# One more pass of lag in a normed attention whose token-major rows have two buffers

## What is computed

```python
qkv = (x @ qkv_w + qkv_b)            # 12 heads of 64
q = layernorm(q, q_norm_w, q_norm_b) # over the 64 features of a head
k = layernorm(k, k_norm_w, k_norm_b)
attn = softmax(q * scale @ k.T)      # 36 x 36 for each head and image
o = (gates[..., None] * (attn @ v)).reshape(B, N, H * HD)
return o @ proj_w + proj_b           # added to the stream h
```

## Time and profile before

| | |
|---|---|
| median of 3 runs | 762.44 us (762.32 to 763.35) |
| the profiled execution, its own time | 763.16 us |
| its span | 761.4 us |
| A1, from token_major(0) to turn(stage + 1, 0) | 271.5 to 390.9 us of the span |
| mean granted TensorE clock | 0.946 of full speed |
| busy: PE, DVE, ACT, POOL | 708.0, 494.7, 345.8, 164.4 us |

### The profile page before, as it was taken

How to read it: one execution, slowest core, us unless ns; L and a number is a source line. 1 busy time by engine, 2 the same in 40 slices (tenths; PEclk the granted TensorE clock), 3 DMA queues, 4 the chain that set the end, 5 groups by cost and what they waited for, 6 DMA issues and landing times.

```text
span 761.4 us, 15938 instructions
## 1 busy us (share of the span) xinstructions
PE 708.0 (93%) x6222; PEld 626.6 (82%) x6222; DVE 494.7 (65%) x1231; ACT 345.8 (45%) x800; POOL 164.4 (22%) x164
## 2 busy tenths in 40 slices
PE   7799999999998799899899998999999999999996
PEld 6588898999985666688776787889999867789996
DVE  1748478888777836466553674478666768456784
ACT  0257354555452133576423432355544545247653
POOL 1200036444242021334111000016443220000000
PEclk9899999999999879899799997999999999769998
DMA  9912022223220000000200010032130200112100
GB/s 263 251 55 79 2 56 77 77 77 104 94 64 0 1 0 2 2 2 1 96 1 1 2 43 2 1 100 58 58 114 23 86 1 3 50 38 74 36 22 24
DMA packets 16200, 38.81 MB, mean 51 GB/s; under 512 B 3577, under 2 KB 4569, under 8 KB 15740
## 3 DMA queue, kind: packets, MB, share of 16 engines
q1 hardware_dynamic: 14150, 36.71, 16.6%
q10 hardware_dynamic: 1976, 1.08, 0.6%
HBM read 37.32 MB, written 0.44 MB: 50 GB/s over the span
## 4 chain that ended last, share of the span: by engine, by line
PE 68%; DVE 20%; issue 4%; POOL 3%; ACT 3%; DMA 1%; POOLq 0%; ACTq 0%; DVEq 0%; SPq 0%
PE PS L711 7%; PE PS L767 5%; PE PS L543 4%; PE PS L547 4%; PE PS L545 4%; PE PS L544 4%; PE PS L546 4%; PE PS L659 4%; PE PS L700 3%; PE PS L595 3%; PE PS L732 2%; POOL ssq L1767 2%; DVE AL L1438 2%; PE PS L596 2%; PE PS L597 2%
## 5 line engine op out<-in xcount | busy, mean ns | idle before, releaser
L936 ACT ACTIVATE MIX<-PS 128x288 f32<-128x288 f32 x118 | 48.5, 411 | 114.8 <-PE PS L547 114.6
L543 PE MATMUL PS<-XH,WH 128*128 128x288 f32 x284 | 87.3, 307 | 2.2 <-DVE OT L1427 1.4
L545 PE MATMUL PS<-XH,WL 128*128 128x288 f32 x284 | 84.7, 298 | 0.0
L544 PE MATMUL PS<-XL,WH 128*128 128x288 f32 x284 | 84.7, 298 | 0.0
L546 PE MATMUL PS<-X,WH 128*128 128x288 f32 x284 | 84.6, 298 | 0.0
L547 PE MATMUL PS<-X,WL 128*128 128x288 f32 x284 | 84.5, 298 | 0.0
L1740 POOL TENSOR_TENSOR rstd<-var,nhalf 96x3 f32<-96x3 f32 x18 | 15.3, 849 | 305.5 <-DVE var L1195 305.5
L1427 DVE TENSOR_TENSOR OT<-MIX,PS 128x288 f32<-128x288 f32 x94 | 42.3, 451 | 39.7 <-ACT MIX L936 39.0
L1438 DVE TENSOR_TENSOR AL<-OT,AH 128x288 fp32r<-128x288 f32 x118 | 59.0, 508 | 3.3 <-ACT AH L950 2.3
L1281 DVE TENSOR_TENSOR WL<-RG,WH 128x768 fp32r<-128x768 f32 (+2 forms) x46 | 57.9, 1258 | 4.4 <-ACT WH L916 4.3
L595 PE MATMUL PS<-AH,DW 128*128 128x288 f32 x166 | 52.6, 317 | 7.2 <-DVE AL L1438 7.0
(11 more groups left out here) (234 smaller groups left out, 1687.8 us busy)
## 6 DMA issues: line engine op xcount, KB each, us to landing
RG<-in_gu_l0f_dram SPq DMA_DIRECT2D x8, 512.0 KB, 4.6
RG<-in_gu_l0f_dram SPq DMA_DIRECT2D x16, 256.0 KB, 5.7
RG<-in_gu_l2f_dram SPq DMA_DIRECT2D x9, 384.0 KB, 3.5
RG<-in_gu_l2f_dram SPq DMA_DIRECT2D x18, 192.0 KB, 4.3
RD<-in_wd_l0f_dram SPq DMA_DIRECT2D x8, 384.0 KB, 3.2
RD<-in_wd_l2f_dram SPq DMA_DIRECT2D x9, 288.0 KB, 2.8
RD<-in_wd_l3f_dram SPq DMA_DIRECT2D x6, 384.0 KB, 3.2
BIG<-in_patch_dram SPq DMA_DIRECT2D x6, 288.0 KB, 7.5
```

What stands on the lines that cost most here:

```text
L543: mm(o, WH[r][:, 0, w], XH[:, cols], start=True, stop=False)
L544: mm(o, WH[r][:, 0, w], XL[:, cols], start=False, stop=False)
L545: mm(o, WL[r][:, 0, w], XH[:, cols], start=False, stop=False)
```

## The change

The lag of the normed attention becomes 2, in the loops of all three engines, and on DVE normalised_heads moves from behind shift to the front of the next pass. The number of TX buffers stays 2 (the diff's new field txs is not read anywhere). The A1 loop has 18 passes; first_out stays 13, since it is the larger of 6 + 2 + 4 and 12 + 1. The other attentions keep their lag and order.

DVE's order in pass i is then: normalised_heads(i - 1), mean_square(i), shift(i - 3), norm(i - 4). PE does qk(i - 2), scores(i - 3), turn_probs(i - 5) and mix(i - 6) in pass i. ScalarE's copy of unit i into TX[i % 2] waits, as before, for qk(i - 2); that is now a step of the same pass.

```diff
         self.paired = dim == 16
-        self.lag = 1 if token_major else 0
+        self.lag = 2 if qk_norm else 1 if token_major else 0
+        self.txs = 2 if qk_norm else 2
...
                     act.wait_ge(S["qk_ready"], u0 + u - 1)
                     activation(TX[u % 2][:, :], PSF[0:TP, 1024:1024 + TAU * 256], ACT.Copy).then_inc(S["tm_taken"], 1)
 
-                lag = 1 if a.tm else 0
+                lag = a.lag
                 for i in range(a.units + lag + 4):
...
-                lag = 1 if a.tm else 0
+                lag = a.lag
                 for i in range(a.units + lag + 4):
+                    if a.qk_norm and 1 <= i <= a.units:
+                        normalised_heads(i - 1)
                     if a.qk_norm and i < a.units:
                         mean_square(i)
...
                     if 0 <= i - lag - 1 < a.units:
                         shift(i - lag - 1)
-                    if a.qk_norm and i < a.units:
-                        normalised_heads(i)
                     if a.gated and i == 0:
                         gates(a)
                     if 0 <= i - lag - 2 < a.units:
```

## The result

The first comparison gave 758.9 us as the median of four executions of the changed kernel (752.72, 752.96, 764.84, 770.68) beside 762.58 for the kernel before; the ratio is 0.9871, with a 95% interval of 0.9847 to 0.9894. Executions of one kernel here can differ by 17 us and more, and each ratio in this text leaves out those that lie over 1.5% above the shortest of their kernel, so it is a ratio of the shorter ones of each group; medians are given beside it, over all executions.

A forecast was written before the change was run, and what follows sets the result against it. The prediction held that a DVE-POOL loop set A1's settled passes (5.68 us, PE 5.15). Its terms, -2.6 - 5.0 - 6.8 + 5.1 + 3.9 = -5.4, took the profiled 763.16 to 757.8, median 757.0; range 753.2 to 761.6.

The forecast's parts named there:

- Settled passes, -2.6: token_major(6) to (11): five passes fall from 5.68 to 5.15 us, PE instead of the DVE-POOL loop setting the pace; -2.6 us.
- The new wait, 0: ScalarE's copy into TX waits for qk of its own pass; in settled passes 0.3 us of cover, no cost.
- The lock on POOL's side: DVE's norm beside POOL's power: its last two instructions may wait, making DVE's loop 5.04 us, still below PE's 5.15.
- Rival 3: Settled passes: DVE still sets the pass because POOL holds up more of norm; 759.6 us, chance 0.08.
- The start, -5.0: A1's first passes: token_major(3) starts at 306.1 instead of 309.85, token_major(6) at 325.6 instead of 330.63; -5.0 us.
- The end, -6.8: token_major(11) to the first output's end: 17.3 us instead of 24.1, if the clock stays up; -6.8 us.
- what would show it: Signs listed for right or wrong, among them settled passes of 5.15 us and the output's first end near 367.
- rival 1: Passes 11 to 13: the clock also falls there, costing 4 us; time 761.0, chance 0.22.
- rival 4: Slower: the clock stays at 1.2 GHz from pass 12 until A2's value products; all of it gives 766.5, chance 0.07.
- Behind the output, +5.1 and +3.9: First output's end to the turn into A2: waits for norm(10) and norm(11) cost +5.1, a low clock there +3.9 us.
- The sum: All terms together: -5.4 us, from the profiled 763.16 to 757.8, or 757.0 as the median.

The follow-up runs named there:

- experiment 11: The changed kernel run once more, no edit against it: median 763.5 us, ratio 0.9874 to the kernel before; its profiled execution took 752.6.
- experiment 4: The changed kernel with three TX buffers instead of two, so the copy waits for qk(i - 3): median 764.7 us, ratio 0.9941; profiled execution 763.2.
- Experiment 7: The changed kernel with first_out 14 instead of 13, the first output one pass later: median 760.1 us, ratio 0.9895.
- experiment 5: The kernel before, with unread matmuls filling PE's waits ahead of qk(1) (24) and qk(11) (22): median 756.1 us, ratio 0.9905.
- experiment 6: The changed kernel with unread matmuls ahead of qk(0), token_major(3), qk(10), qk(11), turn_probs(10) and turn_probs(11): median 749.6 us, ratio 0.9825.
- experiment 1: The changed kernel run again, no edit against it: median 770.9 us, ratio 1.0117 to the kernel before.
- experiment 3: The kernel before with lag 2 in all three loops, DVE's old order kept: median 767.5 us, ratio 1.0079.
- experiment 8: The changed kernel with first_out 14 and unread matmuls ahead of qk(0), token_major(3), qk(10), qk(11): median 754.9 us, ratio 0.9864.
- experiment 12: The changed kernel with first_out 14, unit 0 normed ahead of the gates, unread matmuls ahead of token_major(3), qk(10), qk(11): median 746.3 us, ratio 0.9795.

## Why the prediction was right and wrong

*Settled passes, -2.6.* Right. From token_major(6) to (11) experiment 11 takes 26.0 instead of 28.4: -2.4. PE is the chain.

*The new wait, 0.* Right within 0.16 us, by experiment 4.

*The lock on POOL's side.* It did not occur. In experiment 11's timeline norm's last two instructions run during the power and keep their length:

```profile
341.37 2.26 POOL L1768 TENSOR_TENSOR ssq<-ssq,nhalf 96x12 f32<-96x12 f32 x1 [2.95 <-DVE ssq L1574]
...
342.77 0.17 DVE L1620 TENSOR_TENSOR sm<-sm,GH 72x8 f32<-72x8 f32 x1
...
342.97 0.46 DVE L1625 TENSOR_TENSOR PN<-ES,sm 72x288 f32<-72x288 f32 x1
```

Both have two SBUF inputs; L1620 and L1625 took at most 0.17 and 0.46 in the whole execution. The Trainium skill's rule ("SBUF — State Buffer", section "SBUF: two separate sides") would have held L1620 back to 343.6; here the measurement decides against it, for a power over 12 elements in a row. Rival 3 falls with it.

*The start, -5.0.* Measured -4.6 (325.99 against 330.63). The wait of 1.94 and the start at 306.06 are within 0.2; token_major(3) met the low clock for 4.40 - 2.67 = 1.7 instead of 1.4.

*The end, -6.8.* The step that failed is its condition, "This needs the clock to stay up through passes 11 to 13, where only small matmuls run". Where it held (experiment 11), from token_major(11) to the output's end took 17.4 against 17.3 forecast, with the output itself at 5.98 against 5.9. (The forecast of 367 for that end, under what would show it, does not fit its own sum: 383.15 less 5.0, 2.6 and 6.8 is 368.7; it came at 369.4.) Where it did not (experiment 4), 23.2, so the term shrinks to -0.9. The same wait of 0.77 in the same place was followed by a low clock in one execution and not in the other. I had rival 1 at 4 us and a chance of 0.22. It cost 5.8 in experiment 4, and eleven of 16 executions of the changed kernel have a mean clock at or below 0.939; that all eleven owe it to this place is not shown. Only two of them have a profile; both show this fall, and both lost still more ahead of A1 (5.8 and 5.5 us against the profile of before). These two are also close to what rival 4 describes, at a chance of 0.07: the clock was at 0.50 in 366 to 378 and in 386 to 395, with the upper level in between, and A1's part came out 1.6 longer than before.

*Behind the output, +5.1 and +3.9.* Together 9.0; measured 384.51 - 369.41 - 7.7 = 7.4 in experiment 11 and 390.98 - 375.21 - 7.7 = 8.1 in experiment 4. The waits were 1.43 and 2.39, or 1.70 at the lower clock. The mechanism was right: the layer norm in front of norm(11). Experiment 7 removes it.

*The sum.* For A1 -5.4 was forecast; -6.4 came in experiment 11 (387.00 against 393.38), and +0.1 in experiment 4. On top of that, the same program behind A1 took 761.4 - 393.4 = 368.0 us before and in experiment 4, but 750.8 - 387.0 = 363.8 in experiment 11. This is why the shortest executions, at 752.6, lie below the range, which began at 753.2, and 5.2 below the 757.8 that the sum gives from the profiled execution: A1 gave 1.0 more than forecast, and the stages behind it 4.2, for which the sum has no term. The prediction had named the later stages' clock and put it at nothing. Why those stages came out shorter stays open: the program there is the same, and over all profiles they took 362.1 to 368.2. So one term of the clock failed in each direction, the level in passes 11 to 13 for the long executions and the later stages for the short ones; that 757.0 lies between the two was luck. About half of the forecast gain (-1.8 of the start, -4.9 of the end, +3.9 behind the output: -2.8 of -5.4) was clock and not schedule, and I took it as fixed by the schedule, while the kernel before itself varies by 17 us with it. With the clock held by filled waits, the schedule is worth 3 to 4 us. Its parts, from experiment 5 to experiment 6, fit the forecast's with the clock taken out:

| part | forecast, without its clock | experiment 6 less 5 |
|---|---|---|
| token_major(1) to (6) | -3.2 | -3.0 |
| token_major(6) to (11) | -2.6 | -2.4 |
| to the output's end | -1.9 | -2.7, and -1.0 for 5's low stretch |
| to A2's value products | +5.1 | +4.9 |

## What to carry to other kernels

When a stage waits for a microsecond or less among small matmuls, the clock belongs in the forecast as a spread and not as one number: run the kernel before many times first, and compare stages, by profile, at equal granted clock. A lag added to a hand-written loop moves everything that is tied to a fixed pass number; here the first output slid ahead of the last scores, and putting it back was worth as much as the settled passes (2.5 us with the clock held, against 2.4) and more where the clock was low. Filling PE's waits with idle work is a cheap test of what a low clock costs, and, where nothing better is at hand, a gain.

## What the runs showed of the hardware

The level of the clock in a stretch is not fixed by the program: experiments 4 and 11 agree to 0.02 us from 325.98 to 358.04 and then differ, 0.50 against 1.00 for 10 us, after the same wait of 0.77; experiments 1 and 11, one and the same program, differ there too. The waits of PE ahead of a fall were far shorter than the 3.1 to 3.4 of the rows before: 0.77 in experiment 4, 0.28 and 0.30 in experiment 3, 0.24 and 0.22 in experiment 5. The executions of the kernel before spread over 17 us of 760, those of the changed one over 19, and their mean clock with them. Where the waits at both ends of A1 were filled (experiments 5, 6, 8, 12), the upper level held from pass 2 to A2's value products but for a short stretch in experiment 5. A power on POOL did not delay VectorE, although one line of it took up to 1.05 us instead of 0.45 in the stage where POOL multiplies.
